# Moving the outer tap columns of the offset sums with SBUF transfers instead of matmuls, and a narrower ninth sampling piece

## The chip, the core and the metric

The kernel runs on one core of one Trainium2 chip. The metric is device time in microseconds (us) of one execution. TensorE is called PE here, ScalarE ACT, VectorE DVE, GpSimd POOL and SyncE SP; ACTq and SPq are the sequencers of ACT and SP, which issue transfers.

## The reference, cut to what matters

Two layers of a "metaformer" on x of shape (4, 128, 128, 128), all float32. The change touches only the first half of the first layer: a channel norm, then a deformable 3x3 convolution.

```python
x = x + deform(_ln_c(x), w_off, w_conv)
# deform:
offset = conv3x3(xn, w_off)                    # 18 channels: 9 taps x (dy, dx)
py, px = base_y + dy, base_x + dx
sampled = bilinear_gather(xn, py, px)          # 9 samples for each pixel
out = einsum("bckhw,ock->bohw", sampled, w_conv)
# then: softmax-routed mixture of 8 matrices, a second (spectral) mixing, an expert layer
```

## The kernel before

`phase_a` does norm and deformable convolution in 128 strips of four image rows (32 for each of four images), with image column x on the partitions for the offsets. Every engine walks through one list, `order_a()`, and carries out its own stages of it; the list's slots decide the order on each engine, and semaphores the time. A step takes 12 slots (18 for the last strip of an image, which has six row centres instead of four). In step s the list handles strip F = s + 4 (norm and offset products), Z = s + 2 (offset sums), N = s + 1 (bilinear weights), s (sampling) and s - 2 (the convolution proper).

The stages that the change and the prediction name:

- `turn` (PE, L350), `stats` (DVE), `scale` (POOL), `norm` (ACT, L437), `norm_out` (ACTq, L446, `xtp<-a_tn`, to HBM): the normed strip.
- `conv` (PE, L361) and `y_out` (ACT, L464): 162 products for each pixel: 3 tap rows x 3 tap columns x 18 channels, in `yr`.
- `zsum` (POOL, L589 and L595): sums the three tap rows into `zz`, which still holds three tap columns `kx`.
- `shift` (PE, L374): tap columns 0 and 2 must be moved by one pixel, that is by one partition. Two matmuls with shifted identities add them up in PSUM (`OF`); each float32 matmul is two instructions in the profile.
- `offs` (DVE, L517): adds the middle column; the offsets are then in `on`. `offs_out` (ACTq, L450, `offd<-a_on`) stores them.
- `place` and `hats` (POOL, L623, L607, L610), `bend` (ACT, L473), `clip` (DVE, L528): bilinear hats `hh` from the offsets.
- `prod` (DVE L536, POOL L576) and `turn_s` (DVE, L545): weights `sx`, turned into `tt`, four for each strip.
- `window` (SPq, L658, `a_win<-xtp`): 16 transfers for each strip, each of 8 partitions with 9 runs of 512 bytes.
- `sample` (PE, L405): for every four row centres ("quad") three thirds h = 0, 1, 2 of three pieces each; a piece is 8 matmuls, four row groups of 32 partitions times two window halves. 144 columns for a quad of four centres and 72 for one of two. Third h uses PSUM banks 4 (h % 2) to 4 (h % 2) + 3 and is emptied by `evict` (ACT L482 and DVE L509).
- `out` (PE, L423), `residual` (DVE, L551) and `x1_out` (SPq, `x1d<-a_xo`): the convolution with `w_conv`.

Third h = 1 writes to banks that `turn`, `conv`, `shift` and `out` use too, so PE waits there for their readers:

```python
if h == 1:
    w.wait_ge(normed, convs)
    w.wait_ge(mv_ready, convs // 2)
    w.wait_ge(y_ready, 2 * convs)
    w.wait_ge(on_ready, shifts)
    w.wait_ge(x1_ready, outs)
else:
    w.wait_ge(taken_act, 3 * Q + h // 2)
    w.wait_ge(taken_dve, 3 * Q + h // 2)
```

Of the kernel before, what the change touches and what calls it, by code (L numbers as in the profile page):

```python
# [10 lines left out]
ALU = mybir.AluOpType  # L11
# [4 lines left out]
NG = B * H // 4  # L16
# [30 lines left out]
def setup_phase(nc, ctx, ins, k):  # L47
    sem = lambda n: ctx.enter_context(nc.semaphore("s_" + n))
    filled, loaded, w_in, summed, centred = (
        sem(n) for n in ("filled", "loaded", "w_in", "summed", "centred"))  # L50
    T = ctx.enter_context(nc.psum_tensor("s_t", [128, 162], F32))

    with nc.Block() as block:
        @block.vector
        def _(e):
            e.memset(k["mhalf"][:, :], -0.5)
            e.memset(k["ones"][:, :], 1.0).then_inc(filled, 1)
            e.memset(k["zero"][:, :], 0.0)
# [12 lines left out]
        @block.sync  # L71
        def _(e):
            e.dma_start(k["wraw"][:, :], ins["wof"][:, :]).then_inc(w_in, 16)
            e.dma_start(k["ident"][:, :], ins["ident"][:, :]).then_inc(loaded, 16)
            e.dma_start(k["shift"][:, :, :], ins["shift"][:, :, :]).then_inc(loaded, 16)
# [3 lines left out]
            e.wait_ge(loaded, 80)  # L79
            e.wait_ge(w_in, 16)  # L80
    retire(nc, (filled, loaded, w_in, summed, centred))
# [79 lines left out]
def order_a():  # L161
# [4 lines left out]
    def put(slot, *stage):  # L166
        at.setdefault(slot, []).append(stage)
# [11 lines left out]
    for s in range(-4, NG + 3):  # L179
# [64 lines left out]
def phase_a(nc, ctx, ins, k, xtp, offd, x1d):  # L244
# [6 lines left out]
    zz = S("a_zz", [128, 2, 4, 3, 18])  # L251
# [12 lines left out]
    OF = SB[:, 6, 324:396].rearrange("p (r f) -> p r f", r=4)  # L264
# [4 lines left out]
    def sem(name):  # L269
# [4 lines left out]
    turned, convolved, shifted, sampled, conv_out = (  # L274
        sem(n) for n in ("turned", "convolved", "shifted", "sampled", "conv_out"))
# [3 lines left out]

    filled, bn_done, mv_ready, on_ready, reached, clipped, weighed_dve, turned_s, x1_ready = (  # L280
# [51 lines left out]
    def tensor(e):  # L332
        w = Once(e)

        convs = shifts = outs = taken = 0
# [6 lines left out]
        for o in order:  # L342
# [9 lines left out]
            elif o[0] == "conv":  # L352
# [11 lines left out]
            elif o[0] == "shift":  # L364
                G = o[1]
                bank_free()
                w.wait_ge(z_step, z_count[G])

                w.wait_ge(on_ready, G)
                w.wait_ge(y_ready, 2 * convs)  # L370
                shifts += 1

                for kx in (0, 2):
                    t = e.matmul(OF[:, :, :], k["shift"][:, kx, :], zz[:, G % 2, :, kx, :], start=(kx == 0),  # L374
                                 stop=(kx == 2))
                t.then_inc(shifted, 1)
            elif o[0] == "sample":
# [8 lines left out]
                for h in range(3):  # L386
                    if h == 1:

                        w.wait_ge(normed, convs)
                        w.wait_ge(mv_ready, convs // 2)  # L390
                        w.wait_ge(y_ready, 2 * convs)
                        w.wait_ge(on_ready, shifts)
                        w.wait_ge(x1_ready, outs)
                    else:
                        w.wait_ge(taken_act, 3 * Q + h // 2)
                        w.wait_ge(taken_dve, 3 * Q + h // 2)
                    for i in range(NWIN // 3):
                        for j in range(2):
                            for q in range(4):
# [3 lines left out]
                                m = bass.AP(m.tensor, m.offset, [list(m.ap[0]), [96, 3 * m_], [31, 3], [1, NU_]])  # L403
                                d = SB[:, 4 * (h % 2) + q, 0:432].rearrange("p (k t x) -> p k t x", k=12, t=3)
                                t = e.matmul(d[:, 0:3 * m_, :, NU_ * i:NU_ * i + NU_],  # L405
# [23 lines left out]
    def scalar(e):  # L429
        w = Once(e)  # L430
        for o in order:
# [20 lines left out]
            elif o[0] == "y_out":  # L452
                _, G, h = o
                b, q = divmod(G, GI)
                for r in (2 * h, 2 * h + 1):
# [12 lines left out]
                    a.then_inc(y_ready, 1)  # L468
            elif o[0] == "bend":
# [15 lines left out]
    def vector(e):  # L485
        w = Once(e)
        e.memset(oc[:, :], 0.0)
        e.memset(sx[:, :, :, :], 0.0)
        e.memset(tt[:, :, 2304:2306], 0.0).then_inc(filled, 1)
        for o in order:  # L490
# [20 lines left out]
            elif o[0] == "offs":  # L511
                G = o[1]
                w.wait_ge(shifted, G + 1)
# [3 lines left out]
                e.tensor_tensor(on[:, G % 2, :, :], OF[:, :, :], zz[:, G % 2, :, 1, :], ALU.add).then_inc(on_ready, 1)  # L517
# [35 lines left out]
    def gpsimd(e):  # L553
        w = Once(e)
        for o in order:
# [1192 lines left out]
def program(nc, ins, out, dbg):  # L1748
    with ExitStack() as ctx:
# [38 lines left out]
def constants():  # L1788
    ident = np.eye(128, dtype=np.float32)
    shift = np.zeros((128, 3, 128), np.float32)  # L1790
    for kx in range(3):
        x = np.arange(max(0, 1 - kx), min(128, 129 - kx))
        shift[x + kx - 1, kx, x] = 1.0
# [16 lines left out]
    return {"io": io, "rev": rev, "ident": ident, "shift": shift, "cx": np.ascontiguousarray(cx), "cy": np.ascontiguousarray(cy), "base": base, "far": far}  # L1810
# [41 lines left out]
```

## Time and profile before

| what | value |
|---|---|
| median of three executions | 3882.41 us (3878.23 to 3882.80) |
| the profiled execution | 3885.28 us, its span 3883.5 us |
| PE, busy share of the span | 94% |
| DVE, ACT, POOL, busy share | 76%, 40%, 38% |
| mean granted TensorE clock | 0.956 of full |
| end of `phase_a` (its last PE block) | about 1991 us |

The span runs from the first to the last instruction of the program; the profiled execution's time is 1.8 us longer. `phase_a` takes the first half. A busy share is an average over all stages; matmul ends are modelled, so starts of successive blocks are the better clock on PE.

### The profile page before, as it was taken

The numbers are of one execution on the slowest core, as the hardware profiler recorded it, in microseconds if no ns is written. First come the engines' busy times: TensorE is split into PE (matmuls) and PEld (weight loads), VectorE is DVE, ScalarE is ACT, GpSimd is POOL, SyncE is SP. The second block draws the span as 40 slices with busy tenths as digits, with TensorE's granted clock in tenths as the row PEclk, the third lists the DMA queues.
The fourth block names the chain that finished last, engine by engine and source line by source line (L and its number), as shares of the span: only waits on it lengthen the run. The fifth ranks groups of instructions, "written<-read, shape, count | busy, mean of one in ns | idle before, by whom it ended". The sixth has DMA issues, their size and how long they took to land. (4 is left out here: it accounts for less than half of the span.)

```text
span 3883.5 us, 89684 instructions
## 1 busy us (share of the span) xinstructions
PE 3661.0 (94%) x31447; PEld 2461.6 (63%) x31447; DVE 2944.5 (76%) x9683; ACT 1568.3 (40%) x4561; POOL 1473.4 (38%) x2661
## 2 busy tenths in 40 slices
PE   5999999999999999999979999999999999996567
PEld 4777777777777777777745666666666666654345
DVE  4666666666666666666648999999999999996534
ACT  3444444444444444444411434344334434444124
POOL 4444444444444444544412333333333333333210
PEclk7999999999999999999979999999999999998755
DMA  5655555555555554555527777777777777884689
GB/s 106 108 95 106 103 94 97 97 105 106 90 99 96 107 104 94 96 97 96 88 82 264 272 275 275 268 273 276 274 270 270 277 275 269 282 311 162 249 311 392
DMA packets 611682, 709.87 MB, mean 183 GB/s; under 512 B 62257, under 2 KB 494257, under 8 KB 594849
## 3 DMA queue, kind: packets, MB, share of 16 engines
q1 hardware_dynamic: 505760, 630.17, 58.2%
q10 hardware_dynamic: 104448, 71.85, 5.9%
q8 instruction: 252, 4.13, 0.5%
q0 software_dynamic: 1024, 2.10, 0.2%
q14 instruction: 198, 1.61, 0.2%
HBM read 521.20 MB, written 181.63 MB: 181 GB/s over the span
## 5 line engine op out<-in xcount | busy, mean ns | idle before, releaser
L423 PE MATMUL a_sb<-a_sr,wcv 128*128 128x512 f32 (+3 forms) x2820 | 1052.2, 515 | 0.8 <-DVE a_xo L551 0.8
L405 PEld LDWEIGHTS a_sb<-a_tt,a_win 32*128 32x128 f32 x19008 | 646.5, 186 | 120.8 <-issue 120.1
L423 PEld LDWEIGHTS a_sb<-a_sr,wcv 128*128 128x128 f32 x2820 | 492.8, 190 | 334.2 <-issue 289.2
L405 PE MATMUL a_sb<-a_tt,a_win 32*128 32x144 f32 x19008 | 678.9, 295 | 22.4 <-DMA a_win<-xtp 9.0
L1171 DVE TENSOR_TENSOR b_P<-b_P,b_x 128x1024 f32<-128x1024 f32 x512 | 619.8, 1212 | 0.0
L509 DVE COPY a_sr<-a_sb 128x432 f32<-128x432 f32 (+14 forms) x1172 | 419.2, 412 | 208.6 <-PE a_sb L405 208.6
L482 ACT COPY a_sr<-a_sb 128x432 f32<-128x432 f32 (+14 forms) x1172 | 362.9, 389 | 360.8 <-PE a_sb L405 360.8
L1074 PE MATMUL b_z<-b_P,b_ew 128*128 128x512 f32 x1024 | 463.3, 595 | 0.0
L1077 PE MATMUL b_z<-b_P,b_ew 128*128 128x512 f32 x1024 | 460.3, 592 | 0.0
L1300 POOL TENSOR_TENSOR b_ss<-b_st 128x12 f32<-128x12 f32 (+2 forms) x139 | 30.0, 216 | 1049.7 <-DVE b_pp L1245 963.0
L545 DVE STREAM_TRANSPOSE a_tt<-a_sx 128x576 f32<-128x576 f32 x520 | 398.4, 767 | 14.2 <-POOL a_sx L576 5.4
L576 POOL TENSOR_TENSOR a_sx<-a_hh 128x576 f32<-128x576 f32 x260 | 307.5, 1183 | 126.8 <-DVE a_tt L545 123.4
L551 DVE TENSOR_TENSOR a_xo<-a_sb,a_xin 128x512 f32<-128x512 f32 x128 | 88.3, 690 | 345.5 <-PE a_sb L423 345.5
L1077 PEld LDWEIGHTS b_z<-b_P,b_ew 128*128 128x128 f32 x1024 | 194.6, 190 | 194.1 <-issue 188.0
L1074 PEld LDWEIGHTS b_z<-b_P,b_ew 128*128 128x128 f32 x1024 | 189.0, 195 | 185.3 <-issue 185.3
L1316 POOL TENSOR_TENSOR b_rs<-b_ss,mhalf 128x12 f32<-128x12 f32 (+2 forms) x139 | 301.9, 2172 | 11.1 <-POOL b_ss L1312 0.4
L437 ACT ACTIVATE a_tn<-a_sb,a_rs 128x128 f32<-128x128 f32 x512 | 192.5, 456 | 216.5 <-POOL a_rs L568 216.5
L473 ACT ACTIVATE a_hh<-a_hh 128x576 f32<-128x576 f32 (+1 forms) x128 | 88.3, 690 | 462.4 <-POOL a_hh L610 462.4
L1144 ACT ACTIVATE c_tn<-c_x,b_rs 128x128 f32<-128x128 f32 x512 | 163.7, 391 | 241.9 <-POOL b_rs L1316 241.7
L464 ACT ACTIVATE a_yr<-a_sb,zero,a_rs 128x162 f32<-128x162 f32 (+2 forms) x594 | 226.5, 467 | 57.0 <-ACT a_tn L437 57.0
L623 POOL COPY a_oc<-a_on 128x72 f32<-128x72 f32 x112 | 28.9, 258 | 552.8 <-DVE a_on L517 552.8
L361 PEld LDWEIGHTS a_sb<-wof,a_xin 128*128 128x128 f32 x1024 | 170.5, 194 | 85.4 <-issue 58.1
(184 smaller groups left out, 5343.2 us busy)
## 6 DMA issues: line engine op xcount, KB each, us to landing
b_P<-pd SPq DMA_DIRECT2D x128, 2048.0 KB, 7.8
a_win<-xtp SPq DMA_DIRECT2D x2144, 36.0 KB
a_xin<-in_x SPq DMA_DIRECT2D x128, 256.0 KB, 6.0
xtp<-a_tn ACTq DMA_DIRECT2D x128, 256.0 KB, 2.3
x1d<-a_xo SPq DMA_DIRECT2D x128, 256.0 KB, 5.7
b_x<-x1d SPq DMA_DIRECT2D x128, 256.0 KB, 7.7
x2d<-b_xa SPq DMA_DIRECT2D x128, 256.0 KB, 3.5
pw<-x3d SPq DMA_DIRECT2D x128, 256.0 KB
```

The lines of the kernel that those rows point to most:

```text
L405: t = e.matmul(d[:, 0:3 * m_, :, NU_ * i:NU_ * i + NU_], win[32 * q:32 * q + 32, half_of(Q, j) % NWH, NWIN // 3 * h + i, :], m, start=(j = ...
L423: t = e.matmul(ob[:, r:r + m, :], k["wcv"][:, 3 * (2 - kr) + kx, :], rows[:, :, t_, :], start=(t_ == 0 and r == 0), stop=(t_ == 8))
L437: a = e.activation(tn[:, G % NTN, r, :], TK[:, r, :], ACT.Identity, bias=rs[:, G % 2, r:r + 1], scale=rs[:, G % 2, 4 + r:5 + r])
L464: a = e.activation(yr[:, d:d + 216 * m].rearrange("p (k f) -> p k f", f=216)[:, :, 0:54], YB[r // 2][:, r % 2, 54 * kr:54 * (kr + m)].rear ...
L482: a = e.copy(d, v)
L509: a = e.tensor_copy(d, v)
L545: e.transpose(tt[:, Q % NTP, 0:2304].rearrange("p (j a t x) -> p a t j x", j=2, a=4, t=9)[:, n - quad(Q)[0]], sx[:, n % NST, :, :].rearran ...
L576: e.tensor_tensor(sx[:, n % NST, :, 0:NI * NJ].rearrange("p t (j i) -> p t j i", j=NJ), hh[:, G % 2, i, :, None, 0:NI].to_broadcast([128, ...
L1074: e.matmul(ZE[u][:, :, :], ew[:, x, :], P[:, G % NPB, :, x, :], start=(x == 0), stop=False)
L1077: e.matmul(ZE[u][:, :, :], ew[:, x, :], P[:, G % NPB, :, x, :], start=False, stop=False)
L1171: t = e.tensor_tensor(v, v, x1[:, G % NX1, r, None, :].to_broadcast([128, 8, 128]), ALU.mult)
L1316: e.tensor_tensor(rs[:, u, c], ss[:, u, 2, c], k["mhalf"][:, c], ALU.pow).then_inc(scaled, 1)
```

## The change

The two shift matmuls, their constant (192 KB loaded at the start) and the PSUM part `OF` go. `zz` is laid out with the tap column outermost, so that one tap column of a strip is 72 contiguous floats in each partition. Stage `shift` now issues two transfers from SBUF to SBUF on ACT's queue, each of 127 partitions with 288 bytes: column 0 moved up by one partition, column 2 moved down, into `zs`. `offs` becomes two additions on DVE. The piece 9 of a quad computes only tap columns 1 and 2 and image columns 0 and 1 of its four: 48 columns instead of 144. The slots of several stages move.

```diff
@@ order_a
-                t = t0 + gap * i - 3
+                t = t0 + gap * i - 1
                 put(t, "prod", 2 * p)
-        if 0 <= Z < NG:
-            put(t0 + 4, "shift", Z)
-            put(t0 + 4, "offs", Z)
...
-            put(t0 + 8, "y_out", F, 0)
-            put(t0 + 9, "y_out", F, 1)
+            put(t0 + 9, "y_out", F, 0)
+            put(t0 + 10, "y_out", F, 1)
         if 0 <= Z < NG:
-            put(t0 + 1, "zsum", Z)
-            put(t0 + 5, "offs_out", Z)
-            put(t0 + 5, "place", Z)
-            put(t0 + 5, "hats", Z)
-            put(t0 + 6, "bend", Z)
-            put(t0 + 7, "reach", Z)
-            put(t0 + 7, "clip", Z)
+            put(t0 - 1, "zsum", Z)
+            put(t0 + 2, "shift", Z)
+            put(t0 + 5, "offs", Z)
+            put(t0 + 7, "place", Z)
+            put(t0 + 7, "hats", Z)
+            put(t0 + 7, "offs_out", Z)
+            put(t0 + 8, "bend", Z)
+            put(t0 + 8, "reach", Z)
+            put(t0 + 10, "clip", Z)
@@ tensor
-                for kx in (0, 2):
-                    t = e.matmul(OF[:, :, :], k["shift"][:, kx, :], zz[:, G % 2, :, kx, :], start=(kx == 0),
-                                 stop=(kx == 2))
-                t.then_inc(shifted, 1)
...
-                                m = bass.AP(m.tensor, m.offset, [list(m.ap[0]), [96, 3 * m_], [31, 3], [1, NU_]])
+                                t0, nx = (1, 2) if 3 * h + i == NWIN - 1 else (0, NU_)
+                                m = bass.AP(m.tensor, m.offset + 31 * t0,
+                                            [list(m.ap[0]), [96, 3 * m_], [31, 3 - t0], [1, nx]])
@@ scalar
+            elif o[0] == "shift":
+                G = o[1]
+                w.wait_ge(z_step, z_count[G])
+                w.wait_ge(filled, 1)
+                w.wait_ge(on_ready, G - 1)
+                e.dma_start(zs[1:128, G % 2, 0, :, :], zz[0:127, G % 2, 0, :, :]).then_inc(shifted[G % 2], 16)
+                e.dma_start(zs[0:127, G % 2, 1, :, :], zz[1:128, G % 2, 2, :, :]).then_inc(shifted[G % 2], 16)
@@ vector, offs
-                w.wait_ge(shifted, G + 1)
+                w.wait_ge(shifted[G % 2], 32 * (G // 2 + 1))
+                w.wait_ge(z_step, z_count[G])
...
-                e.tensor_tensor(on[:, G % 2, :, :], OF[:, :, :], zz[:, G % 2, :, 1, :], ALU.add).then_inc(on_ready, 1)
+                e.tensor_tensor(on[:, G % 2, :, :], zs[:, G % 2, 0, :, :], zz[:, G % 2, 1, :, :], ALU.add
+                                ).then_inc(on_half, 1)
+                w.wait_ge(on_half, G + 1)
+                e.tensor_tensor(on[:, G % 2, :, :], on[:, G % 2, :, :], zs[:, G % 2, 1, :, :], ALU.add
+                                ).then_inc(on_ready, 1)
```

On ACT, from the second eviction of a quad on (`a_sr` are evictions, `a_hh` is `bend`, `a_tn` is `norm`), the program before has:

```order
L482 COPY a_sr<-a_sb 128x4x3x3x12
L482 COPY a_sr<-a_sb 128x4x3x2x8 [waits a_sampled]
L482 COPY a_sr<-a_sb 128x4x3x2x9
L482 COPY a_sr<-a_sb 128x4x3x2x10
L450 DMA offd<-a_on 128x72 [waits a_on_ready]
L473 ACTIVATE a_hh<-a_hh 128x576 [waits a_hats_ready]
L437 ACTIVATE a_tn<-a_sb,a_rs 128x128 [waits a_tn_out1,a_rs_step]
L437 ACTIVATE a_tn<-a_sb,a_rs 128x128 x3
L446 DMA xtp<-a_tn 128x4x128 [waits a_normed]
```

And the changed program, at the same place:

```order
L474 COPY a_sr<-a_sb 128x4x3x3x12
L459 DMA a_zs<-a_zz 127x72 [waits a_z_step]
L460 DMA a_zs<-a_zz 127x72
L474 COPY a_sr<-a_sb 128x4x3x2x8 [waits a_sampled]
L474 COPY a_sr<-a_sb 128x4x3x2x9
L474 COPY a_sr<-a_sb 128x4x3x2x10
L422 ACTIVATE a_tn<-a_sb,a_rs 128x128 [waits a_tn_out1,a_rs_step]
L422 ACTIVATE a_tn<-a_sb,a_rs 128x128 x3
L435 DMA offd<-a_on 128x72 [waits a_on_ready]
L431 DMA xtp<-a_tn 128x4x128 [waits a_normed]
L465 ACTIVATE a_hh<-a_hh 128x576 [waits a_hats_ready]
```

The two transfers stand behind the second eviction, `norm` goes ahead of the store of the offsets, and the store of the normed strip behind it. On DVE, from the end of the third eviction on, the program before has:

```order
L509 COPY a_sr<-a_sb 128x4x3x2x10
L536 TENSOR_TENSOR a_sx<-a_hh 128x576 [waits a_turned_s]
L545 STREAM_TRANSPOSE a_tt<-a_sx 128x9x2x32 [waits a_weighed_dve]
L517 TENSOR_TENSOR a_on<-a_sb,a_zz 128x72 [waits a_oc_ready,a_reached,a_on_out0,a_shifted]
L496 BN_STATS a_st<-a_sb 128x6 [waits a_rs_step,a_turned]
L496 BN_STATS a_st<-a_sb 128x6 x3
L499 BN_AGGR a_mv<-a_st 128x2 [waits a_bn_done] x4
L545 STREAM_TRANSPOSE a_tt<-a_sx 128x9x2x32 [waits a_weighed_pool]
```

And the changed program, from the same eviction to the start of the next step (`a_xo` is `residual`):

```order
L489 BN_STATS a_st<-a_sb 128x6 x3
L492 BN_AGGR a_mv<-a_st 128x2 [waits a_bn_done] x4
L534 TENSOR_TENSOR a_sx<-a_hh 128x576 [waits a_turned_s]
L511 TENSOR_TENSOR a_on<-a_zs,a_zz 128x72 [waits a_oc_ready,a_on_out0,a_reached,a_z_step,a_shifted0]
L514 TENSOR_TENSOR a_on<-a_on,a_zs 128x72 [waits a_on_half]
L543 STREAM_TRANSPOSE a_tt<-a_sx 128x9x2x32 [waits a_weighed_dve]
L543 STREAM_TRANSPOSE a_tt<-a_sx 128x9x2x32 [waits a_weighed_pool]
L520 TENSOR_REDUCE fm<-a_on 128x1 [waits a_on_ready]
L521 TENSOR_REDUCE fm<-a_on 128x1
L526 TENSOR_SCALAR a_hh<-a_hh 128x576 [waits a_bent]
L534 TENSOR_TENSOR a_sx<-a_hh 128x576 [waits a_turned_s,a_clipped]
L549 TENSOR_TENSOR a_xo<-a_sb,a_xin 128x512 [waits a_x1_out0,a_conv_out]
```

The statistics go ahead of the offsets; behind the addition that waits for the transfers (`a_shifted0`) stand the strip's last two `turn_s`, `clip`, a product and the residual.

## Rows read from the trace of the kernel before

**Rows 1.** Windows, one long stretch of `phase_a`: length, busy time of each engine.
```profile
600.00:1000.00 400.00, 399.20 (x4841) 286.76 (x4843) 272.14 (x727) 179.64 (x472) 198.06 (x323) 1.00 0.55 100
```
**Rows 2.** PE's waits, 200 to 1900 us: total us, times, longest.
```profile
PE a_sb L405 <- DVE a_sr L509: 2.8, 3, 0.9
```
**Rows 3.** Timeline of PE over one strip: start us, length us, instructions.
```profile
1047.34 5.10 PE L405 MATMUL a_sb<-a_tt,a_win 32*128 32x144 f32 x144
1052.36 0.67 PE L374 MATMUL a_sb<-a_zz,shift 128*128 128x72 f32 x4
1052.87 0.60 PE L350 MATMUL a_sb<-ident,a_xin 128*128 128x128 f32 x4
...
1062.22 5.08 PE L405 MATMUL a_sb<-a_tt,a_win 32*128 32x144 f32 x144
```
**Rows 4.** Timeline of PE, a quad of two centres near the end.
```profile
1970.18 4.25 PE L405 MATMUL a_sb<-a_tt,a_win 32*128 32x72 f32 x144
1974.37 1.99 PE L423 MATMUL a_sb<-a_sr,wcv 128*128 128x256 f32 x8
```
**Rows 5.** Timeline of PE, the shifts on both sides of an image's last strip.
```profile
1002.32 0.67 PE L374 MATMUL a_sb<-a_zz,shift 128*128 128x72 f32 x4
...
1022.55 0.67 PE L374 MATMUL a_sb<-a_zz,shift 128*128 128x72 f32 x4
```
**Rows 6.** Timeline of DVE, ACT and POOL over the strip of rows 3.
```profile
1049.30 0.95 ACT L482 COPY a_sr<-a_sb 128x288 f32<-128x288 f32 x3 [1.26 <-PE a_sb L405]
1050.91 0.97 ACT L482 COPY a_sr<-a_sb 128x432 f32<-128x432 f32 x2 [0.66 <-PE a_sb L405]
...
1054.87 0.20 DVE L517 TENSOR_TENSOR a_on<-a_sb,a_zz 128x72 f32<-128x72 f32 x1
1055.10 0.37 ACTq L450 DMA_DIRECT2D offd<-a_on  x1
1055.13 0.24 POOL L623 COPY a_oc<-a_on 128x72 f32<-128x72 f32 x1 [5.06 <-DVE a_on L517]
1056.84 0.68 ACT L473 ACTIVATE a_hh<-a_hh 128x576 f32<-128x576 f32 x1 [3.50 <-POOL a_hh L610]
1057.55 0.46 DVE L528 TENSOR_SCALAR a_hh<-a_hh 128x576 f32<-128x576 f32 x1 [0.51 <-ACT a_hh L473]
1058.05 0.76 DVE L536 TENSOR_TENSOR a_sx<-a_hh 128x576 f32<-128x576 f32 x1
1062.33 0.69 DVE L551 TENSOR_TENSOR a_xo<-a_sb,a_xin 128x512 f32<-128x512 f32 x1 [2.71 <-PE a_sb L423]
```
**Rows 7.** DMA view, 200 to 1900 us: queues (packets, MB, share of 16 engines' time), issues (count, KB, median us to landing).
```profile
q1 hardware_dynamic: 184168, 130.93, 46.3%
q10 hardware_dynamic: 75422, 33.54, 7.4%
...
a_win<-xtp SPq DMA_DIRECT2D x1880, 36.0 KB
x1d<-a_xo SPq DMA_DIRECT2D x113, 256.0 KB, 5.7
xtp<-a_tn ACTq DMA_DIRECT2D x112, 256.0 KB, 2.3
```
**Rows 8.** Tile `a_on`, 200 to 1900 us, the store of the offsets.
```profile
DMA to landing us min/median/max: 2.1/5.5/9.7
```
**Rows 9.** DMA view of 1052.34 to 1057.34 us, while windows load.
```profile
q1 hardware_dynamic: 770, 0.36, 57.6%
```
**Rows 10.** Windows: DMA share and GB/s in the last two columns, while windows load and while 128-row transfers run.
```profile
1052.40:1053.80 1.40, 1.40 (x14) 1.16 (x11) 1.29 (x4) 0.84 (x3) 0.00 (x0) 1.00 0.41 97
1047.34:1048.34 1.00, 1.00 (x29) 1.00 (x32) 0.90 (x2) 0.70 (x2) 0.86 (x2) 1.00 1.14 240
```
**Rows 11.** Windows of PE near the start: busy us, granted clock.
```profile
74.00:80.00 6.00, 1.66 (x48) 0.85 0.23 62
80.00:85.00 5.00, 5.00 (x88) 0.50 0.52 71
```

More of the change, by code:

```diff
@@ L74, in _ @@
             e.dma_start(k["ident"][:, :], ins["ident"][:, :]).then_inc(loaded, 16)
-            e.dma_start(k["shift"][:, :, :], ins["shift"][:, :, :]).then_inc(loaded, 16)
             e.dma_start(k["wcv"][:, :, :], ins["wcv"][:, :, :]).then_inc(loaded, 16)
@@ L78, in _ @@
             e.dma_start(k["cy"][:, :, :], ins["cy"][:, :, :]).then_inc(loaded, 16)
-            e.wait_ge(loaded, 80)
+            e.wait_ge(loaded, 64)
             e.wait_ge(w_in, 16)
@@ L206, in order_a @@
             put(t0 + 4, "stats", F)
-            put(t0 + 6, "scale", F)
             put(t0 + 5, "conv", F, 0)
             put(t0 + 6, "conv", F, 1)
+            put(t0 + 6, "scale", F)
             put(t0 + 7, "norm", F, 0)
@@ L250, in phase_a @@
     yr = S("a_yr", [128, NYR * 162 + 216])
-    zz = S("a_zz", [128, 2, 4, 3, 18])
+    zz = S("a_zz", [128, 2, 3, 4, 18])
+    zs = S("a_zs", [128, 2, 2, 4, 18])
     on = S("a_on", [128, 2, 4, 18])
@@ L271, in sem @@
         return sems[-1]
-    turned, convolved, shifted, sampled, conv_out = (
-        sem(n) for n in ("turned", "convolved", "shifted", "sampled", "conv_out"))
+    turned, convolved, sampled, conv_out = (
+        sem(n) for n in ("turned", "convolved", "sampled", "conv_out"))
+    shifted = [sem(f"shifted{i}") for i in range(2)]
     normed, y_ready, bent, taken_act = (sem(n) for n in ("normed", "y_ready", "bent", "taken_act"))
     taken_dve = sem("taken_dve")
+    on_half = sem("on_half")
     filled, bn_done, mv_ready, on_ready, reached, clipped, weighed_dve, turned_s, x1_ready = (
@@ L333, in tensor @@
         w = Once(e)
-        convs = shifts = outs = taken = 0
+        convs = outs = taken = 0
         def bank_free():
@@ L363, in tensor @@
                 t.then_inc(convolved, 1)
[L364 to L371, printed above, removed]
-                for kx in (0, 2):
-                    t = e.matmul(OF[:, :, :], k["shift"][:, kx, :], zz[:, G % 2, :, kx, :], start=(kx == 0),
-                                 stop=(kx == 2))
-                t.then_inc(shifted, 1)
             elif o[0] == "sample":
@@ L401, in tensor @@
                                 m = tt[32 * q:32 * q + 32, Q % NTP, 1152 * j + u:1152 * j + u + 1]
[L403 removed]
+                                t0, nx = (1, 2) if 3 * h + i == NWIN - 1 else (0, NU_)
+                                m = bass.AP(m.tensor, m.offset + 31 * t0,
+                                            [list(m.ap[0]), [96, 3 * m_], [31, 3 - t0], [1, nx]])
                                 d = SB[:, 4 * (h % 2) + q, 0:432].rearrange("p (k t x) -> p k t x", k=12, t=3)
[L405 removed]
+                                t = e.matmul(d[:, 0:3 * m_, t0:3, NU_ * i:NU_ * i + nx],
                                              win[32 * q:32 * q + 32, half_of(Q, j) % NWH, NWIN // 3 * h + i, :], m,
@@ L488, in vector @@
         e.memset(sx[:, :, :, :], 0.0)
+        e.memset(zs[:, :, :, :, :], 0.0)
         e.memset(tt[:, :, 2304:2306], 0.0).then_inc(filled, 1)
@@ L582, in gpsimd @@
                 q = G % GI
-                v = yr[:, 4 * G % NYR * 162:(4 * G % NYR + 4) * 162].rearrange("p (r k f) -> p r k f", r=4, k=3)
-                z = zz[:, G % 2, :, :, :].rearrange("p r k f -> p r (k f)")
+                v = yr[:, 4 * G % NYR * 162:(4 * G % NYR + 4) * 162].rearrange("p (r k x f) -> p r k x f", r=4, k=3, x=3)
+                z = zz[:, G % 2, :, :, :].rearrange("p x r f -> p r x f")
                 n = z_count[G]
@@ L1766, in program @@
             SA = lambda name, shape, dt=F32: ca.enter_context(nc.sbuf_tensor(name, shape, dt))
-            k |= {"zero": SA("zero", [128, 640]), "wof": SA("wof", [128, 162]), "shift": SA("shift", [128, 3, 128]), "wcv": SA("wcv", [128, 9, 128]),
+            k |= {"zero": SA("zero", [128, 640]), "wof": SA("wof", [128, 162]), "wcv": SA("wcv", [128, 9, 128]),
                   "cx": SA("cx", [128, 9, NI]), "cy": SA("cy", [128, 14, NJ])}
@@ L1789, in constants @@
     ident = np.eye(128, dtype=np.float32)
[L1790 to L1793, printed above, removed]
     x, t, i = np.arange(128)[:, None, None], np.arange(9)[None, :, None], np.arange(NI)[None, None, :]
@@ L1809, in constants @@
     rev = np.ascontiguousarray(ident[:, (128 - np.arange(128)) % 128])
-    return {"io": io, "rev": rev, "ident": ident, "shift": shift, "cx": np.ascontiguousarray(cx), "cy": np.ascontiguousarray(cy), "base": base, "far": far}
+    return {"io": io, "rev": rev, "ident": ident, "cx": np.ascontiguousarray(cx), "cy": np.ascontiguousarray(cy), "base": base, "far": far}
 OUTN = ["out"]
```

4 lines of the change are left out of this document (removed).

## The prediction

> **What bounds the kernel now.** I read the windows first. In 400 us from the middle of `phase_a` PE is busy 399.2 us, DVE 272, ACT 180 and POOL 198 [rows 1]. The list of PE's waits agrees: over 1700 us its longest entry is 2.8 us [rows 2]. So before the change only PE's own work sets this phase. The timeline gives the step: samples start at 1047.34 and 1062.22, a period of 14.88 us [rows 3]; the last strip of an image takes 1022.55 - 1002.32 = 20.2 us [rows 5]. Every other engine has slack, so the first question is what PE saves, and the second whether a new chain becomes longer than PE's step. Granted clock is 1.00 in rows 1.
>
> **What PE saves.** The shift block runs from 1052.36 to 1052.87, 0.51 us [rows 3]; 128 strips give 65 us. The ninth piece: a sample of 144 instructions takes 5.02 us from its start to the next block at 144 columns [rows 3], 34.9 ns each, and 4.19 us at 72 columns [rows 4], 29.1 ns each. Half the columns save 5.8 ns only, so these matmuls don't go by columns. For 16 instructions of 48 columns the bounds are nothing and, by columns, 16 x 34.9 x 2/3 = 0.37 us; I take the measured 16 x 5.8 ns = 0.09 us, 12 us over 128 quads (the four short quads are already at the lower rate). PE alone would need 14.28 us for a step, and the kernel would end at 3885 - 65 - 12 = 3808 us. The constant no longer loaded is worth under 1 us.
>
> **What it adds elsewhere.** Second addition: 0.20 us of DVE [rows 6], with 4.8 us of DVE idle in each step (14.88 x (1 - 272.1/400)) [rows 1]: hidden. Two issues on ACTq of 0.37 us each [rows 6], ahead of the third eviction, which PE needs only in the next step: hidden. Two transfers of 127 rows of 288 bytes: this is the term that decides.
>
> **How long the transfers may take.** A loop runs from one pair's landing to the next pair's issue. I follow it with durations of rows 6. Landing to first addition 0.1 (estimate); the additions 0.2 + 0.06 + 0.2, where one stood, so 0.25 more than before; first addition to end of product, as now, 1054.87 to 1058.05 + 0.76 = 3.94; residual 0.69, with 0.05 of gap. That is 5.0 us. The sample's third h = 1 waits for `x1_ready`, the residual, and may start then. An eviction starts 1.96 us after its third does (1049.30 - 1047.34), and takes 0.97 us on ACT; the transfers stand right behind it. So 8.0 us from landing to issue, and the period is 8.0 + L, L being the time from first issue to last landing. It stays hidden up to L = 14.28 - 8.0 = 6.3 us. `turn_s` for the next quad ends 2.2 us after landing and binds later than this loop. Behind the waiting addition on DVE stand two `turn_s`, `clip`, the product and the residual, so PE is late twice, before h = 0 and h = 1.
>
> **How long they take.** No row shows a transfer of 127 rows. Neighbours: 128 rows of 2 KB (512 packets of 512 bytes) on ACT's queue land in 2.3 us [rows 7]; 128 rows of 288 bytes, issued while windows load, in 5.5 us median, 2.1 to 9.7 [rows 8]. If the 127 rows were spread over all engines as these are, L would be 2.1 to 5.5 and a little, hidden. But transfers with few rows aren't spread so. While windows alone load (8 partitions each), the DMA share is 0.41 and 97 GB/s, against 1.14 and 240 GB/s with 128-row transfers [rows 10], though 770 packets in 5 us are outstanding work throughout [rows 9]; 0.41 x 16 is 6.6 engines. And the issue list gives a landing for the 128-row transfers and none for the windows [rows 7]. I read this as equal shares: rows are cut into equal numbers for each engine, 16 x 8 for 128, 8 x 1 for 8. 127 is prime and has no such cut but 127 x 1 or 1 x 127.
>
> The Trainium skill states this as a rule (DMA: Bandwidth & Descriptors, "Why a DMA increments its semaphore by 16 and not by 1"): a hardware-queue copy uses the largest number of engines up to 16 that divides its row count, the lowest-numbered ones, and 127 partitions go to a single engine. By the rule the change makes a hidden transfer into the bound; the trace agrees as far as 8 and 128 rows go, and no run here shows 127.
>
> So one DMA engine, one of those that load windows, moves 254 packets per strip. Their price: ACT's queue has 75422 packets in 7.4% of 16 x 1700 us, 26.7 ns each [rows 7]: 6.8 us for 254. Upper bound by SP's queue, 46.3% and 184168 packets, 68 ns [rows 7]: 17.4 us. Fixed part: the 2.3 us less 32 packets x 27 ns = 1.4 us. Work in the way: for each strip that engine also gets 144 window packets, 16 of `x1d` and `a_xin`, and their marks, about 178; 770 packets in 5.0 us over eight engines are 52 ns each [rows 9], 9.3 us. Windows start once the normed strip has landed: that store now stands behind the offsets' store, so at landing + 0.6 + 0.4 + 2.3 = 3.3 us, moving from about 4.2. Until our first packet at about 8.9, 4.7 us of the 9.3 are gone and 4.6 are left, and rings that share an engine take turns. L = 1.4 + 6.8 + 4.6 = 12.8 and the period is 20.8 us. Check by load alone: 9.3 + 42 x 0.027 + 6.8 = 17.2 us per strip on that engine, a floor above 14.88. The 26.7 ns hold packets that waited, so 20.8 is rather high; I take 19.5 us, between the two.
>
> **The sum.** 123 ordinary steps x (19.5 - 14.88) = +568 us; the four long steps, 20.2 us already, about 0; PE's savings lie beside the wait and count for nothing. 3885 + 568 = 4453; the profiled execution lies 3 us above the median, so 4450.
>
> **Rivals.**
> 1. *All 16 engines, hidden (faster).* L = 2.1 to 5.5 us, below 6.3, and the savings stand: 3805 us. It needs 127 rows to be spread unequally; it decides at L under 6.3. Against it: rows 10. Chance 0.06.
> 2. *One engine, but windows out of its way.* L = 1.4 + 6.8 = 8.2, period 16.2, 3885 + 123 x 1.3 = 4047; with turns that favour our ring up to 17.2, 4170. For it: the window issue can shift to where the transfers are done. Chance 0.18.
> 3. *One engine and dearer packets or a slower clock.* At 68 ns throughout L = 18.8, period 26.8, 5350 us. Or PE's clock falls: with PE busy 1.66 of 6 us near the start the next stretch runs at 0.50, that is 1.2 GHz [rows 11]; in the loop only h = 1 (1.6 us) doubles, +1.6 us a step or 200 us. Chance for 4750 and more 0.14.
> 4. *Transfers just hidden.* L near 6.9 gives 14.9 us, no change within 0.2%, which is about what a measurement of this kernel can tell. Chance 0.02.
> 5. *My forecast*, 17.2 to 21.8 us a step, 4170 to 4740 us: 0.60.
>
> **The numbers.** Range 4030 to 4850: it takes in rival 2 and the lower part of 3, and leaves out the fast case, no change, and steps over 22.7 us. Faster by over 0.2% 0.06, same 0.02, slower 0.92.
>
> **What would show it.** In the changed profile: (a) L374 is gone and the sample is about 0.1 us shorter to the next block; (b) PE has waits of some 2 to 5 us a strip, before the sample and before its second third, named after `a_tt` and `a_xo` of DVE; (c) DVE's idle time ahead of the first addition (L511) is large, ended by DMA `a_zs`; (d) `a_zs` lands over 10 us after issue, and the issue list gives it no median, as with the windows; (e) the normed strip's store lands later than 2.3 us; (f) `phase_a` ends near 2560 us, the rest is unchanged. I am wrong if the transfers land within 6 us (then it is 3805), or if ACT doesn't reach the issue 8 us after landing.

## The result, and the profile after

| | before | after |
|---|---|---|
| median | 3880.96 us of four (3878.23 to 3882.80) | 4516.87 us of four (4509.33 to 4535.27) |
| ratio of after to before | | 1.1643 (95%: 1.1624 to 1.1661) |
| mean granted TensorE clock | 0.956 | 0.906 |
| last PE block of `phase_a` | about 1991 us | about 2625 us |

The change makes the kernel 16% slower; 4450 us was predicted. The profiled execution took 4518.43 us, its span 4516.6 us. `phase_a` ends 634 us later, and that is the whole difference (4518 - 3885 = 633). In the experiments, e2, e3, e5, e6 and e7 are one execution each, the others medians of four to eleven; the executions of one kernel lie within 0.6% of each other.

From the page: busy time of the engines, the granted clock in 40 slices, and two groups (after the first bar busy us and mean ns of one, after the second the idle time just before them and what ended it).

```profile
PE 3804.6 (84%) x30935; PEld 2582.2 (57%) x30935; DVE 2931.0 (65%) x9812; ACT 1549.2 (34%) x4561; POOL 1549.2 (34%) x2661
...
PEclk7899898998988989989998989999999999999765
...
L390 PE MATMUL a_sb<-a_tt,a_win 32*128 32x144 f32 (+1 forms) x19008 | 869.2, 346 | 509.7 <-issue 400.1
...
L511 DVE TENSOR_TENSOR a_on<-a_zs,a_zz 128x72 f32<-128x72 f32 x128 | 30.2, 236 | 988.6 <-DMA a_zs<-a_zz 988.6
```

PE stood idle 510 us ahead of its samples, and DVE 989 us ahead of the first addition, every bit of it ended by the transfers into `a_zs`. The window of [rows 1] and the list of waits of [rows 2], this time from 200 to 2500 us (total us, times, longest), after:

```profile
600.00:1000.00 400.00, 318.35 (x3539) 233.06 (x3538) 196.08 (x578) 128.52 (x376) 152.44 (x234) 0.89 0.41 75
```
```profile
DVE a_on L511 <- DMA a_zs<-a_zz: 876.2, 115, 13.6
...
PE a_sb L390 <- issue: 354.1, 107, 9.1
...
ACT a_sr L474 <- issue: 244.3, 69, 5.1
...
PE a_sb L390 <- DVE a_xo L549: 69.2, 74, 3.2
```

PE is busy 318 us of 400 where it was 399. It waits once before the sample and once before its second third. The first wait is put down to "issue": the profile names no releaser for it, though in the program's order the sample there waits for `turn_s`, which stands on DVE behind the addition. The mean clock is 0.89 where it was 1.00, and the sample of 6.51 us below shows where it is lost. Windows of its first third and of the rest (length, busy time of PE, clock):

```profile
1203.11:1206.15 3.04, 3.04 (x48) 0.50 0.37 111
1206.15:1209.55 3.40, 3.40 (x100) 0.95 0.60 75
```

After 4.3 us without work PE begins the sample at 0.50, the lower level (1.2 GHz), and the first third takes 3.04 us, against 5.1 us for a whole sample before. Early in the second third the clock is back at 1.00. One strip on the timeline (start us, length us, in brackets the idle time before and what ended it):

```profile
1201.16 0.23 DVE L511 TENSOR_TENSOR a_on<-a_zs,a_zz 128x72 f32<-128x72 f32 x1 [8.88 <-DMA a_zs<-a_zz]
1201.43 0.23 DVE L514 TENSOR_TENSOR a_on<-a_on,a_zs 128x72 f32<-128x72 f32 x1
...
1203.11 6.51 PE L390 MATMUL a_sb<-a_tt,a_win 32*128 32x144 f32 x144 [4.30 <-issue]
...
1205.33 0.68 DVE L549 TENSOR_TENSOR a_xo<-a_sb,a_xin 128x512 f32<-128x512 f32 x1
...
1208.24 0.54 ACT L474 COPY a_sr<-a_sb 128x432 f32<-128x432 f32 x1 [0.86 <-PE a_sb L390]
1208.25 0.63 ACTq L459 DMA_DIRECT2D a_zs<-a_zz  x1
1208.91 0.61 ACTq L460 DMA_DIRECT2D a_zs<-a_zz  x1
...
1221.16 0.23 DVE L511 TENSOR_TENSOR a_on<-a_zs,a_zz 128x72 f32<-128x72 f32 x1 [8.55 <-DMA a_zs<-a_zz]
1223.11 6.75 PE L390 MATMUL a_sb<-a_tt,a_win 32*128 32x144 f32 x144 [4.08 <-issue]
```

This is the loop of the prediction, closed: addition at 1201.16, residual until 1206.01, the sample's second third from 1206.15, eviction and issue at 1208.25, next addition at 1221.16. A step of 20.0 us is 7.1 us from the addition to the issue and 12.9 us from the issue to the next addition. Over the 115 strips between 200 and 2500 us the median of the first part is 7.4 us, of the second 12.3 us, and of the period 19.9 us.

The trace also records every packet of the transfers with its start, length and size, and these records say more of the second part. The 254 packets of a strip start 3.6 us after the issue (median), the last one ends 8.0 us after the first one starts, and the addition follows 0.7 us later. In none of the 115 strips are more than two of the 254 in flight at once.

### The profile page after: what moved, and what is told of

The parts are those of the page before. It is cut to its first block and busy times, and to the rows that moved or that the text cites. A ratio compares the mean times of both kernels' runs of the same rounds, so it can differ in the third digit from the quotient of the medians.

```text
span 4516.6 us, 89044 instructions
## 1 busy us (share of the span) xinstructions
PE 3804.6 (84%) x30935; PEld 2582.2 (57%) x30935; DVE 2931.0 (65%) x9812; ACT 1549.2 (34%) x4561; POOL 1549.2 (34%) x2661
## 5 line engine op out<-in xcount | busy, mean ns | idle before, releaser
L390 PE MATMUL a_sb<-a_tt,a_win 32*128 32x144 f32 (+1 forms) x19008 | 869.2, 346 | 509.7 <-issue 400.1
L390 PEld LDWEIGHTS a_sb<-a_tt,a_win 32*128 32x128 f32 x19008 | 827.5, 235 | 639.1 <-issue 632.5
L511 DVE TENSOR_TENSOR a_on<-a_zs,a_zz 128x72 f32<-128x72 f32 x128 | 30.2, 236 | 988.6 <-DMA a_zs<-a_zz 988.6
L574 POOL TENSOR_TENSOR a_sx<-a_hh 128x576 f32<-128x576 f32 x260 | 378.0, 1454 | 552.1 <-DVE a_tt L543 385.7
L543 DVE STREAM_TRANSPOSE a_tt<-a_sx 128x576 f32<-128x576 f32 x520 | 386.2, 761 | 1.0 <-POOL a_sx L574 0.5
```

The lines of the kernel that those rows point to most:

```text
L390: t = e.matmul(d[:, 0:3 * m_, t0:3, NU_ * i:NU_ * i + nx], win[32 * q:32 * q + 32, half_of(Q, j) % NWH, NWIN // 3 * h + i, :], m, start=(j ...
L543: e.transpose(tt[:, Q % NTP, 0:2304].rearrange("p (j a t x) -> p a t j x", j=2, a=4, t=9)[:, n - quad(Q)[0]], sx[:, n % NST, :, :].rearran ...
L574: e.tensor_tensor(sx[:, n % NST, :, 0:NI * NJ].rearrange("p t (j i) -> p t j i", j=NJ), hh[:, G % 2, i, :, None, 0:NI].to_broadcast([128, ...
```

## The experiments

Together they ask four things: is it the transfers at all (e6, e7), is it their being on one DMA engine (e1, e2, e3, e5), is it where they stand (e8 to e11), and what is the other half of the change worth (e4). e1 to e3 and e5 to e7 start from the changed kernel, and e4 from the kernel before.

**e1_split: 127 rows cut into 112 and 15.** The same bytes in four issues.

```diff
-e.dma_start(zs[1:128, G % 2, 0, :, :], zz[0:127, G % 2, 0, :, :]).then_inc(shifted[G % 2], 16)
+for p, m in ((0, 112), (112, 15)):
+    e.dma_start(zs[p + 1:p + 1 + m, G % 2, 0, :, :], zz[p:p + m, G % 2, 0, :, :]).then_inc(shifted[G % 2], 16)
```
(and so for the other column; the wait counts 64 instead of 32)

> The changed kernel with each transfer of 127 rows cut into one of 112 and one of 15 rows; all bytes move as before, with four issues in place of two. Theory A (127 rows go to one DMA engine, which also loads windows, and its queue makes the wait): each piece is spread over 15 or 16 engines, lands in 2 to 6 us, the step falls from 20.0 to about 14.3 us and the time to 3800 to 3830 us. Theory B (transfers from SBUF to SBUF with short rows are slow among the window loads, however many engines share them): two more issues and the same bytes, so 4450 to 4600 us. Theory C (the new order is at fault: DVE waits in the list ahead of two turn_s whatever the landing): over 4200 us.

Measured: 4007.2 us, 1.0315 of before (1.0300 to 1.0331). A step is 16.0 us, 8.9 us of it from the first issue to the addition (medians). So 510 of the 636 us go away when the rows are cut differently. The number lies in none of the three ranges: B and C are far off, and A expected landings that would be hidden. What is left shows in two views. The first is the list of waits from 200 to 1900 us, the second the issue list of that stretch (count, KB, median us to landing):

```profile
DVE a_on L513 <- DMA a_zs<-a_zz: 454.7, 105, 6.9
...
ACT a_sr L476 <- issue: 237.7, 105, 3.3
```
```profile
a_zs<-a_zz ACTq DMA_DIRECT2D x211, 31.5 KB, 3.6
...
a_zs<-a_zz ACTq DMA_DIRECT2D x211, 4.2 KB, 5.4
```

The pieces of 15 rows land 5.4 us after their own issue (median), and the four issues hold ACT's third eviction for 2.3 us a strip.

**e2_rows126 and e3_rows113: one row less, 14 rows less.** 126 has large divisors; 113 is a prime like 127.

```diff
# e2
+e.dma_start(zs[1:127, G % 2, 0, :, :], zz[0:126, G % 2, 0, :, :]).then_inc(shifted[G % 2], 16)
+e.dma_start(zs[0:126, G % 2, 1, :, :], zz[1:127, G % 2, 2, :, :]).then_inc(shifted[G % 2], 16)
# e3
+e.dma_start(zs[1:114, G % 2, 0, :, :], zz[0:113, G % 2, 0, :, :]).then_inc(shifted[G % 2], 16)
+e.dma_start(zs[0:113, G % 2, 1, :, :], zz[1:114, G % 2, 2, :, :]).then_inc(shifted[G % 2], 16)
```

> The changed kernel with 126 rows in each of the two transfers in place of 127; one row of each is left out, so one pixel column of the offsets lacks a tap column. Theory A: 126 can be shared equally by 14 engines, so the wait goes, with the same two issues: 3800 to 3840 us. Theories B and C: 1% fewer bytes, 4480 to 4520 us.

> The changed kernel with 113 rows in each transfer; 14 rows of each are left out. 113 is a prime, so by theory A one engine still moves all of it: 28 packets fewer for each strip at 27 ns are 0.75 us off a step of 20.0, 123 steps, so about 4425 us, far slower than with 126 rows. Theory B: by bytes 11% off the wait of 12.9 us, 1.4 us a step, 4340 us. If the number of rows alone mattered (fewer is faster), it would be faster than 126 rows.

Measured: 3861.97 us and 4427.39 us. One row less makes the changed kernel faster than the kernel before; 14 rows less leave it almost as slow as it was. The same strip in e2 on the timeline:

```profile
1208.58 0.83 ACTq L459 DMA_DIRECT2D a_zs<-a_zz  x1
1209.45 1.67 ACTq L460 DMA_DIRECT2D a_zs<-a_zz  x1
...
1217.11 0.23 DVE L511 TENSOR_TENSOR a_on<-a_zs,a_zz 128x72 f32<-128x72 f32 x1 [4.17 <-DMA a_zs<-a_zz]
```

Here it is 8.5 us to the addition, 7.4 us in the median over 114 strips, and the step 15.0 us: with 7.1 us from addition to issue the loop is just longer than PE's 14.3 us. So the wait shrinks but doesn't go, and e2 lies above the 3840 us that was expected. This pair shows that the number of rows decides, and not the amount. The packet records agree with the reading that 127 and 113 rows go to one engine: with 113 rows again never more than two packets of a strip are in flight at once, while the peak of a strip is 9 to 22 packets with 126 rows, and 10 to 22 in e1.

**e5_one_long: column 0 with 127 rows, column 2 with 126.**

```diff
-e.dma_start(zs[0:127, G % 2, 1, :, :], zz[1:128, G % 2, 2, :, :]).then_inc(shifted[G % 2], 16)
+e.dma_start(zs[0:126, G % 2, 1, :, :], zz[1:127, G % 2, 2, :, :]).then_inc(shifted[G % 2], 16)
```

> The changed kernel with column 0 still moved by 127 rows and column 2 by 126 rows (one row left out). Theory A (one engine's queue): that engine moves 127 + 9 packets in place of 254, 3.2 us less, and meets fewer window packets; period 7.1 + L with L between 8.5 (126 rows both) and 12.85 (127 rows both), about 10 us: a step of about 17 us, 4100 to 4200 us. If a transfer of 127 rows were slow for a fixed reason of its own and both ran side by side, one of them would cost as much as two: 4500 us.

Measured: 4158.84 us; the median from issue to addition is 10.4 us, between 7.4 (e2) and 12.3 (after). Each of the two transfers brings its part.

**e6_no_transfers: neither transfers nor the wait for them.**

```diff
-e.dma_start(zs[1:128, G % 2, 0, :, :], zz[0:127, G % 2, 0, :, :]).then_inc(shifted[G % 2], 16)
-e.dma_start(zs[0:127, G % 2, 1, :, :], zz[1:128, G % 2, 2, :, :]).then_inc(shifted[G % 2], 16)
...
-                w.wait_ge(shifted[G % 2], 32 * (G // 2 + 1))
```

> The changed kernel without the two transfers and without DVE's wait for them; the outer tap columns are left out of the offsets. It shows the new order and PE's savings alone. If the transfers' landing is the whole loss: 3881 - 65 - 19 = about 3797 us, PE saturated, step 14.2 us. If the new order itself brings waits: more, up to the 3862 us of 126 rows.

Measured: 3804.11 us, steps of 14.28 to 14.35 us. Windows and PE's timeline, to be held against [rows 1] and [rows 3]:

```profile
600.00:1000.00 400.00, 399.04 (x4981) 287.29 (x4980) 281.08 (x811) 185.00 (x524) 216.05 (x325) 1.00 0.59 104
```
```profile
1043.58 4.95 PE L390 MATMUL a_sb<-a_tt,a_win 32*128 32x144 f32 x144
1048.47 0.65 PE L350 MATMUL a_sb<-ident,a_xin 128*128 128x128 f32 x4
1048.96 1.02 PE L408 MATMUL a_sb<-a_sr,wcv 128*128 128x512 f32 x2
...
1057.88 4.95 PE L390 MATMUL a_sb<-a_tt,a_win 32*128 32x144 f32 x144
```

PE is its own bound again, at 1043.58 to 1057.88 = 14.30 us a step. Everything else of the change (slots, second addition, layout) costs at most a few us (3804 against 3797 expected), and the granted clock is back at 1.00.

**e7_unwaited: the same two transfers, between two tiles that nobody reads, and no wait on DVE.**

```diff
+                w.wait_ge(shifted[G % 2], 32 * (G // 2))
-                e.dma_start(zs[1:128, G % 2, 0, :, :], zz[0:127, G % 2, 0, :, :]).then_inc(shifted[G % 2], 16)
-                e.dma_start(zs[0:127, G % 2, 1, :, :], zz[1:128, G % 2, 2, :, :]).then_inc(shifted[G % 2], 16)
+                e.dma_start(zu[1:128, G % 2, 0, :, :], zk[0:127, G % 2, 0, :, :]).then_inc(shifted[G % 2], 16)
+                e.dma_start(zu[0:127, G % 2, 1, :, :], zk[1:128, G % 2, 2, :, :]).then_inc(shifted[G % 2], 16)
...
-                w.wait_ge(shifted[G % 2], 32 * (G // 2 + 1))
```

> The changed kernel whose two 127-row transfers run between two tiles that nothing else uses, at the same place on ACT's queue, and DVE doesn't wait for them; the outer tap columns are left out of the offsets. It parts the wait from the load on the engine. If DVE's wait is the cost: 3797 to 3830 us, as without transfers. If the load (windows late, ACT held while it issues) costs by itself: 3850 us and more; the loaded engine has 17 us of packets by my count for a step of 14.2, which would show as 4150 us or more.

Measured: 3830.08 us. Three steps in four are 14.28 to 14.35 us, with the same windows and with transfers of the same shape as in the changed kernel. Windows, then queues (packets, MB, share of 16 engines' time) and issues from 200 to 1900 us:

```profile
600.00:1000.00 400.00, 398.00 (x5002) 284.68 (x5004) 277.00 (x799) 182.66 (x519) 213.12 (x328) 1.00 0.49 108
```
```profile
q1 hardware_dynamic: 188589, 133.75, 36.0%
q10 hardware_dynamic: 106523, 42.64, 11.3%
...
xtp<-a_tn ACTq DMA_DIRECT2D x114, 256.0 KB, 6.5
...
a_zu<-a_zk ACTq DMA_DIRECT2D x230, 35.7 KB
...
offd<-a_on ACTq DMA_DIRECT2D x116, 36.0 KB, 6.5
```

The stores behind the transfers on ACT's queue land after 6.5 us instead of 2.3 us [rows 7], and it costs PE little. So the DMA engines, the one that carries the transfers too, keep up with 14.3 us a step as far as throughput goes; what the changed kernel pays for is the latency inside the loop. Of the 26 us between e6 and e7, about 15 are waits of PE for the residual, which e6 doesn't have (200 to 1900 us); why the residual is late in these steps was not followed.

```profile
PE a_sb L392 <- DVE a_xo L552: 14.9, 12, 3.0
```

**e4_ninth: the kernel before with the ninth piece of 48 columns, and nothing else.**

```diff
+                                t0, nx = (1, 2) if 3 * h + i == NWIN - 1 else (0, NU_)
+                                m = bass.AP(m.tensor, m.offset + 31 * t0,
+                                            [list(m.ap[0]), [96, 3 * m_], [31, 3 - t0], [1, nx]])
```

> The kernel before with the ninth piece of a quad at 48 columns alone. By the 72-column quad (29.1 against 34.9 ns an instruction) 16 instructions save 0.09 us a step, 12 us, ratio 0.997. By the undisturbed samples of the changed kernel (4.87 us against 5.02) 0.15 us a step, 20 us, ratio 0.995. By columns it would be 0.37 us a step, 47 us, ratio 0.988.

Measured: 3863.62 us, 0.9951 of before (0.9938 to 0.9965). PE's timeline:

```profile
1052.52 4.96 PE L407 MATMUL a_sb<-a_tt,a_win 32*128 32x144 f32 x144
1057.41 0.67 PE L374 MATMUL a_sb<-a_zz,shift 128*128 128x72 f32 x4
...
1067.27 0.95 PE L407 MATMUL a_sb<-a_tt,a_win 32*128 32x144 f32 x20
```

From the sample to the next block it is 4.89 us where it was 5.02 [rows 3], and the step 14.75 us (1052.52 to 1067.27) where it was 14.88: 0.13 us.

**e8_sp_early: cut into 112 + 15 and issued on SP's queue ahead of the windows, with a looser order behind.**

```diff
-            put(t0 + 2, "shift", Z)
+            put(t0 - 1, "shift", Z)
...
-                t = t0 + gap * i - 1
+                t = t0 + gap * i
...
-                put(t + 1, "turn_s", 2 * p)
-                put(t + gap // 2, "turn_s", 2 * p + 1)
+                put(t + 2, "turn_s", 2 * p)
+                put(t + max(3, gap // 2), "turn_s", 2 * p + 1)
...
-            put(t0 + 8, "bend", Z)
+            put(t0 + 10, "bend", Z)
```
(`offs_out` at + 8, `clip` at + 12 and the residual ahead of the products as well; stage `shift` moves from `scalar` to `sync`)

> All bytes moved, but as 112 and 15 rows, issued on SP's queue right behind the sum of the tap rows and ahead of the window loads, and an order in which the residual and the product for the next quad don't stand between a late landing and PE: residual ahead of clip, sums ahead of products on POOL, bend behind the y copies. If landing time in the loop is the only cost, the step falls to PE's own 14.2 us: 3797 to 3830 us, faster than both kernels. If not, the waits will name what binds next, and it may be over 3880 us.

Measured: 3906.84 us, 1.0068 of before (1.0051 to 1.0085): a miss. Steps vary between 14.3 and 16.6 us with a mean of about 14.85, and there are new waits (200 to 1900 us):

```profile
PE a_sb L391 <- DVE a_sr L496: 26.8, 59, 0.9
PE a_sb L391 <- DMA a_win<-xtp: 14.7, 3, 5.8
```

The transfers are out of the way: DVE waits for them 0.6 us in all. But the order that was to give more room makes DVE's evictions late (27 us), and over the whole kernel PE waits 50 us for windows, 35 of them in one wait; the rest of the 103 us over e6 isn't assigned. Two things went into one kernel here, so the next ones take them apart.

**e9_sp_split and e10_sp_whole: the changed kernel's own order, with `shift` alone moved to SP's queue.** e9 has the cut into 112 and 15, e10 the two uncut transfers of 127 rows.

```diff
-            put(t0 + 2, "shift", Z)
+            put(t0 - 1, "shift", Z)
```

> The changed kernel's own order, with one stage moved: the transfers are issued on SP's queue right behind the sum of the tap rows, so ahead of the window loads of the step, as 112 and 15 rows. By the loop, landing to next issue is 6.6 us (to the end of the second POOL sum) and the landing at most 6 to 7 us with nothing in the way, together under PE's 14.3: steps of 14.3 to 14.4 us, 3800 to 3830 us, faster than the kernel before and than the ninth piece alone (3864). If issue costs or windows that now start later bind, 3850 us or more.

> The same move of the stage to SP's queue, but with the two transfers of 127 rows uncut, so still one engine. Landing alone on that engine by my packet price is 1.4 + 254 x 23 to 27 ns = 7.2 to 8.3 us; 6.6 + 7.2 to 8.3 = 13.8 to 14.9 us against PE's 14.3: 3800 to 3890 us. If one engine is slow whatever lies beside it (the windows in the way were no part of the loss): L stays near 12.9, over 4400 us.

Measured: e9 3853.11 us, 0.9921 (0.9907 to 0.9934), slower than the 3800 to 3830 us expected, though under both kernels; e10 3883.93 us, 0.9998 (0.9989 to 1.0008). With whole 127-row transfers the kernel is 16% slower than before when they are issued on ACT's queue behind the windows, and as fast as before when they stand on SP's queue ahead of them; the 77 us that e6 gains on before are still lost. Queue and place in the step were moved together, so the two aren't told apart. On the timeline of e10:

```profile
1204.04 0.62 SPq L668 DMA_DIRECT2D a_zs<-a_zz  x1
1204.71 1.60 SPq L669 DMA_DIRECT2D a_zs<-a_zz  x1
1206.40 7.02 SPq L649 DMA_DIRECT2D a_win<-xtp  x16
...
1212.39 0.23 DVE L504 TENSOR_TENSOR a_on<-a_zs,a_zz 128x72 f32<-128x72 f32 x1 [2.12 <-DMA a_zs<-a_zz]
```

From issue to addition it is 8.4 us here and 7.8 in the median over 114 strips, and the issue comes 6.55 us after the addition: 14.4 us against PE's 14.3. The packets start 1.3 us after the issue, and the last one ends 5.2 us after the first one starts (medians; 3.6 and 8.0 us in the changed kernel), again with never more than two in flight: it is still one engine, with less in its way. Between issue and first packet a median of 430 window packets start in the changed kernel and none in e10. In e9 nearly all steps are 14.28 to 14.35 us, and its 49 us over e6 lie elsewhere: its first sample starts at 70.5 us (e6: 43.1), and the three steps across an image's border take 9.7, 12.7 and 14.4 us (e6: 5.1 each). PE's list of waits over the whole span names them:

```profile
PE a_sb L390 <- DMA a_win<-xtp: 60.3, 4, 36.2
```

On SP's queue the windows of the first strips now stand behind transfers that wait for `zsum`.

**e11_sp_order: e9, with the first three strips' windows issued early and `shift` one slot later at an image's last strip.** The diff is against the changed kernel; the split and the move to SP's queue are as in e9.

```diff
-            put(t0 + 2, "shift", Z)
+            put(t0 if s % GI == GI - 1 else t0 - 1, "shift", Z)
...
+    early = {steps[w - 3]: w for w in range(3)}
...
+        if slot in early:
+            out.append(("window", early[slot]))
+            windows += 1
```

> The kernel of the split transfers on SP's queue, with two changes to the order on SP alone: the first three windows are issued one for each of the first steps in place of behind the third strip's transfers, and in the last strip of an image the windows go ahead of the transfers. In that kernel the first sample began at 70 us instead of 43, and three samples at image borders waited 24 us in sum for windows. If those are all that is left, 27 + 24 of 51 us come back: 3853 - 51 = 3802 us, as without transfers (3804). If SP's queue is too full at the borders in another way, some of the 24 us stay, 3825 us.

Measured: 3815.45 us, 0.9835 of before (0.9822 to 0.9849). Windows and waits (whole span):

```profile
600.00:1000.00 400.00, 398.94 (x4975) 285.17 (x4974) 282.40 (x814) 184.69 (x523) 216.28 (x332) 1.00 0.59 109
```
```profile
PE a_sb L394 <- DVE a_tt L540: 19.8, 2, 16.3
```

The borders are back at 5.1 to 5.6 us. The first sample starts at 55.9 us, 12.8 us later than in e6, and the kernel ends 11.3 us later. This version computes everything and beats both kernels: 67 us under before, 701 us under the changed one.

## Why the prediction was right, step by step

The sign, the mechanism and the size held: 4450 us against 4517, 1.5% too low.

- **PE's own saving** (14.28 us a step, 3808 us in all): e6 has 14.28 to 14.35 us and 3804 us. The sum is right, one term is not: the ninth piece was taken at 0.09 us and gives 0.13 (e4, 18 us in time instead of 12). The price of 5.8 ns was for 72 columns less, and the piece drops 96; at the same rate that is 16 x 7.7 ns = 0.12 us, an estimate that fits, though no run varies the width. Against that, the `turn` block takes 0.49 us behind a sample (1048.47 to 1048.96), where it took 0.43 behind the shift block (1052.87 to 1053.30).
- **Landing to next issue** (8.0 us): 7.1 us here, 7.4 in the median. The additions, the product and the residual took what was said. The error is the 0.97 us for the eviction: the issue starts at 1208.25, 0.01 us after the eviction's first copy, so ACT's sequencer doesn't wait for the copy to end.
- **Issue to landing** (12.8 us): 12.9 us on the strip shown up to the start of the addition, 12.3 in the median. The two subtotals hold as well: 1.4 + 6.8 = 8.2 us ahead of the windows (e10: 8.4, median 7.8), and 4.5 us more behind them, where 4.6 was taken. Their terms don't, and that the errors cancel is luck. In e10 the fixed part is 1.3 us to the first packet and 1.3 us from the last packet to the addition (medians), 2.6 us where 1.5 was taken (1.4, and the 0.1 us from landing to addition, which stands on no row). The packets take 5.2 us, about 20 ns each, where 26.7 ns were taken. Behind the windows the packets are spaced out to 8.0 us, and the first of them starts 3.6 us after the issue, where the prediction had 0.9 (8.9 against 8.0 us after landing). Transfers that are spread over more engines start after 1.5 us (e2) and 1.3 us (e1) at the same place, so the late start goes with the one engine. That this engine first works off its window packets is the likely reading; the records, which name no engine, don't show it.
- **Averaged down to 19.5 us.** This is the step that failed in size. The loop gave 20.8, and I took less, because the packets seemed dear, and for a "check by load alone" that called 17.2 us a strip a floor. e7 has the same load in 14.3 us, so the sum of packet times that I took for a floor is none. The records show why: packets of one engine overlap. In the strip of e10 that is shown the records of the 254 packets add up to 6.0 us and span 4.8 us, with two in flight for a quarter of that time. The rows of before had a sign of it: 57.6% of 16 engines [rows 9] is 9.2 engines, more than the eight that I gave the windows. Measured are 20.0 us; 123 x (20.0 - 14.88) = 630, and 3885 + 630 = 4515, against 4518 in the profiled execution.
- **One engine for 127 rows.** 126 rows 3862 us, 113 rows 4427, one transfer of each kind 4159, cut into 112 and 15 rows 4007: only the row count separates them, and the packets in flight (two at most with 127 and 113 rows, peaks of 9 and more in e1 and e2) go with it. It is the rule of the Trainium skill (DMA: Bandwidth & Descriptors, "Why a DMA increments its semaphore by 16 and not by 1") that a copy takes the largest number of engines up to 16 that divides its rows. By that rule, 127 and 113 get one engine, 112 gets 16, 15 gets 15 and 126 gets 14, and the times agree. The engine numbers themselves are in no view here.
- **Rival 1** (spread transfers, 2.1 to 5.5 us, hidden at 3805 us): even with 127 rows spread it would not have come in at that price. In the same place of the step e2 needs 7.4 us and e1 8.9 us. The bound of [rows 8] was for a store issued elsewhere in the step. The point from which it decides was set at 6.3 us; with the measured 7.1 us for the other part it is 7.2 us. **Rival 2** (windows out of the way, 16.2 us a step) did happen in e10, with a shorter way to the issue. **Rival 3** (slower clock): the clock does fall to 0.50, in most steps (87 of the 118 samples of 200 to 2500 us have over 1 us of it), but most of it falls on the first third of the sample, which is not in the loop, and in the strip shown it is back at 1.00 early in the second. From the start of the second third to its eviction it is 2.35 us in the median, where it was 1.85 before: 0.5 us more, where the rival had 1.6. The dearer packets (68 ns) didn't come.
- **The signs.** (a) L374 is gone. (b) Both waits are there, the first longer than the second, but the first is named "issue". (c) 988.6 us ahead of L511. (d) `a_zs` has no landing median; but in e2 the 126-row transfers have none either, so a missing median isn't a mark of one engine. (e) Wrong: the normed strip's store lands in 2.4 us (at most 4.8), since ACT reaches it only after the transfers have landed; in e7, where nobody waits for them, it does get late (6.5 us). (f) `phase_a` ends at about 2625 us, not 2560.

What stays open: what exactly delays the first packet of a one-engine transfer behind the windows, whether SP's queue or the place ahead of the windows makes the gain of e10, why the residual is late in some steps of e7, and the first 13 us of e11, which no run takes apart.

## What to carry to other kernels

Before a matmul is replaced by a transfer, write down the loop that the transfer closes (landing to next issue, and issue to landing) and compare it with the step of the engine that sets the pace: with the same bytes and packets, 7.1 + 12.9 us lost 16%, and 6.55 + 7.8 us against 14.3 us of PE only gave back what the change saves. Choose the number of rows of a transfer so that it divides well (a row less, or a cut into 112 and 15), and issue it ahead of the large loads, not behind them. A transfer whose landing has slack may take nearly three times as long at little cost (the normed strip's store in e7: 6.5 us for 2.3), so look at who waits before looking at the load.

## What the runs showed of the hardware

- An issue can be held, and with it the instructions that stand behind it on its engine. Minimum, median and maximum length in ns, from the tile's view of the changed kernel:

```profile
L459 ACTq DMA_DIRECT2D a_zs<-a_zz x115: 626/626/636, 204.9 to 2482.1; - x115
L460 ACTq DMA_DIRECT2D a_zs<-a_zz x115: 607/3102/5397, 205.6 to 2482.7; - x115
```

  ACT's third eviction stands behind the second issue; that is its 244 us of waits for "issue". It isn't the same in every strip (0.61 us in the one shown), and one engine for the transfer isn't enough for it: with 113 rows the second issue takes at most 1.04 us. What holds it is open. Without a hold an issue takes 0.82 us with 126 rows, 0.57 us with 112, 0.85 us with 15 and 0.37 us with 128 [rows 6].
- Where a transfer stands matters as much as how it is cut. The two columns of 36 KB, cut into 112 and 15 rows, have their last packet 8.0 us after the first issue when they are issued on ACT's queue while windows load (e1), and 4.1 us after it on SP's queue ahead of the windows (e9; medians). Uncut, on one engine, it is 11.8 us (after) and 6.5 us (e10).
- Packets of 288 bytes on one engine: 254 of them in 5.2 us (e10, median), never more than two in flight.
- With PE waiting some 4 us a step the granted clock of the long stretch is a mean of 0.89: the sample starts at 0.50 (1.2 GHz) after the wait and PE is at 1.00 (2.4 GHz) again before the sample ends. Without that wait (e6, e11) the stretch is at 1.00.
